# One decoder layer: softplus as four squares, a narrower position bias, and another route from the last batch to its router logits

## The chip, the cores and the metric

The kernel runs on one core of one Trainium2 chip. The metric is the device time of one launch in microseconds (us); lower is better. TensorE (PE in the profile) multiplies matrices, VectorE (DVE) and ScalarE (ACT) do elementwise work, GpSimd (POOL) too, and SyncE (SP) issues most DMAs. Each engine runs its own instructions in order and waits for the others by semaphores.

## The reference, cut to what matters

A post-norm decoder layer over x (4 batches of 256 tokens, width 256) and a context (4 x 256 x 128), in float32.

```
x = layernorm(x + attention(x))          # 32 heads of 8, relative position bias
x = layernorm(x + mamba(context, z=x))   # conv, silu, softplus, scan over 16 states, gate y * silu(x)
# mixture of experts: logits = x @ Wr + br; the best of 4 experts, weighted by its softmax
# expert: (silu(x @ Wg) * (x @ Wu)) @ Wd, 256 -> 1024 -> 256; out = layernorm(x + expert)
```

The position bias of a head is `rel_pos[clip(k - q + 63, 0, 126)].mean()`: it depends on k - q alone and is constant where the distance is 63 or more. The scan's step size is `dt = softplus(v) = relu(v) + log(1 + exp(-|v|))`.

## The kernel before, in words

Every engine has its own program, in an order written out by hand. There are four parts.

The start (0 to 78 us): weights and tokens are turned, queries and keys are projected and written as three bf16 parts each to DRAM (`store_parts`, one call per half of the tokens), from where they come back stacked (`load_stack`, 48 rows a head). Convolution and silu give u, and from that the scan's inputs B, C and dt. VectorE makes the third part of queries and keys (`third_part`, L1351), and then takes the maxima of the first batch's scores (16 units, `maxima`, L1395) with "chores" in between: third parts, `put_u`, and the steps of `softplus(0, step)` (L1374). The logarithm is a polynomial of degree 9 by Horner's rule: one scaling (L1379), eight steps `poly = (poly + c) * e` (L1381) and one addition (L1384), each over 1024 columns, which is half the tokens of both channel blocks. ScalarE's `take_dt` (L1163) makes e = exp(-|v|). After the last chore VectorE clears PSUM (L1564, L1565) and sets `scan_in`, on which ScalarE's first `decay` and GpSimd's first `inject` wait.

The loop (78 to 320 us): 4 batches b of 8 slots qd, each slot for 4 heads and 2 of the batch's 16 scan states m. In a slot TensorE does, four times (i = 0 to 3), the transposed scores of two heads (`scores_b`, L882) and, interleaved, plain scores of two heads of the next half batch, for their maxima (`keys_a` L866, `bias_a` L871). The bias is added by matmuls: `bias_a` multiplies a flip matrix with a Hankel matrix over 512 columns (L872), the bias of `scores_b` is four matmuls of 128 columns, each with its own weights (L901). `weigh` (L907) sums the probabilities times v, `sum_states` (L832) adds a scan state into PSUM by an fp32 identity matmul (L841). ScalarE does the exponentials (L1262) and the scan's decays (L1225). VectorE takes two maxima per state and scans it (L1440); in batch 0, slots 2 to 6, it also does the ten steps of `softplus(1, step)`, for the other half of the tokens. GpSimd multiplies each state's input (`inject`, L608) and output (`weigh_state`, L616), 512 columns each. The eight `tail` steps of a batch (context turned, normalised, projected, added, statistics) run in slots 1 to 4 of the next batch. A unit of TensorE takes the next of two PSUM banks (`turn`) once VectorE has emptied it (`taken`).

The last batch's end (320 to 362 us): `sum_states` ends, then `put_y`, the 8 `tail` steps of batch 3, the scaling (`seed`, `newton`) and `centre` of the first layernorm (L1508), ScalarE's `squash` (L1247), VectorE's `gate` (L1518), `turn_back` (L957), `add_mixed` (L1526), again scaling and `centre`, then the rows are turned (`turn_x2`), copied (`put_x2`) and multiplied with Wr (`route`, `put_logits`). Routing follows on VectorE (L1609 to L1658): one-hot of the best expert, positions by two counting matmuls, a one-hot matrix per token tile (L1647), the row indices. `keep_warm` (L827) issues matmuls without use in between. GpSimd then gathers the rows of 11 tiles (L674) and copies each for TensorE to turn (`hand_row`, `turn_x`).

The experts (362 us to the end): a loop over 11 tiles (L1081 to L1125), which no edit touches.

## Time and profile before

| | us |
|---|---|
| median of 3 runs | 501.59 (497.32 to 502.73) |
| the profiled execution's own time | 503.87 |
| its span, first to last instruction | 501.9 |
| TensorE busy | 448.9 (89%) |
| VectorE busy | 324.1 (65%) |
| GpSimd busy | 222.3 (44%) |
| ScalarE busy | 199.4 (40%) |
| mean granted TensorE clock | 0.954 |

Busy shares are means over parts with different limits, so they have to be read by part. The clock is given as a share of 2.4 GHz: 0.50 is 1.2 GHz. Durations of one instruction include its latency, and neighbours on one engine overlap by some 0.1 us, so the cost of one in a chain is the distance from its start to the next start. The 2 us between span and own time lie outside the instructions.

### The profile page before, as it was taken

What the parts mean: (1) busy time and instruction counts of PE and PEld (TensorE: products, weight loads), DVE (VectorE), ACT (ScalarE), POOL (GpSimd) and SP (SyncE); (2) the same over time, 40 slices, a digit from 0 to 9 for tenths busy, and PEclk for the clock granted to TensorE, in tenths of its full rate; (3) what the DMA queues carried; (4) which work ended last, traced back from release to release, by engine and by line L of the source; (5) the groups of instructions that cost most, each with busy time, mean ns of one, the idle gap of its engine ahead of it and who ended that gap; (6) DMA issues with size and microseconds to landing.
All of it is one profiled execution on the core that took longest, in us unless ns stands there. A gap on an engine that the chain in (4) does not pass through costs nothing.

```text
span 501.9 us, 8238 instructions
## 1 busy us (share of the span) xinstructions
PE 448.9 (89%) x2779; PEld 223.7 (45%) x2780; DVE 324.1 (65%) x621; ACT 199.4 (40%) x392; POOL 222.3 (44%) x239
## 2 busy tenths in 40 slices
PE   5899967977998999999999999878699999999992
PEld 3444222422343444444444443433345665666662
DVE  2696886999987778857888666477302433334344
ACT  1564315645464576635756467211011111121110
POOL 2000109887786789836898579100450111111001
PEclk9999875989899999989999999989989999999997
DMA  8799950243282442914545210394110000000000
GB/s 226 141 233 155 292 178 23 103 90 72 74 143 75 102 99 79 226 52 156 168 166 166 70 44 1 127 368 133 34 51 0 10 10 12 11 10 10 10 2 8
DMA packets 39367, 49.39 MB, mean 98 GB/s; under 512 B 4664, under 2 KB 32673, under 8 KB 39334
## 3 DMA queue, kind: packets, MB, share of 16 engines
q1 hardware_dynamic: 36322, 46.65, 35.0%
q0 software_dynamic: 1056, 2.10, 1.3%
q10 hardware_dynamic: 1956, 0.21, 0.4%
q8 instruction: 20, 0.33, 0.3%
q14 instruction: 13, 0.11, 0.1%
HBM read 40.72 MB, written 8.91 MB: 99 GB/s over the span
## 4 chain that ended last, share of the span: by engine, by line
PE 71%; DVE 17%; issue 5%; POOL 3%; ACT 2%; DMA 1%; POOLq 0%; SPq 0%; DVEq 0%
PE ps L1086 15%; PE ps L841 9%; PE ps L1102 8%; PE ps L872 7%; PE ps L868 7%; PE ps L914 5%; DVE arena L1381 4%; PE ps L901 4%; PE ps L741 3%; DVE arena L1440 3%; DVE arena L1397 3%; PE ps L1094 2%; PE ps L754 1%; PE ps L945 1%; PE ps L953 1%
## 5 line engine op out<-in xcount | busy, mean ns | idle before, releaser
L1262 ACT ACTIVATE arena<-ps 128x512 f32<-128x512 f32 x128 | 76.1, 595 | 101.1 <-PE ps L901 101.0
L1397 DVE TENSOR_REDUCE arena<-ps 128x2 f32<-128x512 f32 x128 | 86.7, 685 | 31.1 <-PE ps L872 28.8
L619 POOL TENSOR_TENSOR arena<-arena 128x512 f32<-128x512 f32 x60 | 76.2, 1270 | 41.5 <-DVE arena L1440 41.5
L613 POOL TENSOR_TENSOR arena<-arena 128x512 f32<-128x512 f32 x64 | 90.5, 1416 | 0.3
L1086 PE MATMUL ps<-arena 128*128 x176 | 79.2, 604 | 0.7 <-ACT arena L1288 0.6
L1440 DVE TENSOR_TENSOR_SCAN arena<-ps,arena 128x512 f32<-128x512 f32 x60 | 72.8, 1213 | 2.3 <-ACT ps L1225 1.2
L841 PE MATMUL ps<-arena,identf 128*128 128x512 f32 x128 | 71.1, 646 | 0.0
L1225 ACT ACTIVATE ps<-arena 128x255 f32<-128x255 f32 x128 | 60.4, 473 | 11.3 <-DVEq L1567 11.3
L868 PE MATMUL ps<-arena 48*128 48x256 bf16 x256 | 51.8, 284 | 14.1 <-ACT arena L1262 7.0
L1665 DVE TENSOR_TENSOR arena<-arena,ps 128x1024 f32<-128x1024 f32 x11 | 13.4, 1221 | 67.9 <-ACT arena L1292 67.9
L872 PE MATMUL ps<-hank_hi,flip 128*128 128x512 f16 x128 | 52.1, 407 | 0.0
L895 PE MATMUL ps<-arena 49*128 49x256 bf16 x256 | 51.2, 281 | 0.1
L901 PE MATMUL ps<-flip,hank 128*128 128x128 f16 x512 | 51.1, 224 | 0.0
L1086 PEld LDWEIGHTS ps<-arena 128*128 128x128 f32 x176 | 33.1, 193 | 39.1 <-issue 39.1
L686 POOL DMA_INDIRECT out<-rows_s,arena x11 | 10.8, 982 | 88.4 <-DVE rows_s L1694 88.4
L868 PEld LDWEIGHTS ps<-arena 48*128 48x128 bf16 x256 | 14.4, 95 | 79.0 <-DVE arena L1397 43.0
L901 PEld LDWEIGHTS ps<-flip,hank 128*128 128x128 f16 x512 | 39.2, 100 | 17.6 <-issue 5.0
L1102 PE MATMUL ps<-arena 128*128 x176 | 39.9, 380 | 1.2 <-ACT arena L1296 1.2
L1292 ACT ACTIVATE arena<-ps 128x1024 f32<-128x1024 f32 x11 | 11.3, 1023 | 67.8 <-PE ps L1086 67.8
L1102 PEld LDWEIGHTS ps<-arena 128*128 128x128 f32 x176 | 32.7, 190 | 5.9 <-issue 1.9
L914 PE MATMUL ps<-arena,vaug 128*9 128x256 f32 x512 | 34.5, 388 | 0.8 <-ACT arena L1262 0.8
L674 POOL DMA_INDIRECT rows_s<-x_d,arena x11 | 11.3, 1031 | 43.4 <-DVEq L1659 40.6
(200 smaller groups left out, 532.9 us busy)
## 6 DMA issues: line engine op xcount, KB each, us to landing
arena<-bc_d SPq DMA_DIRECT2D x32, 512.0 KB, 4.1
arena<-in_L_ffn_Wg SPq DMA_DIRECT2D x8, 512.0 KB, 5.7
arena<-in_L_ffn_Wu SPq DMA_DIRECT2D x8, 512.0 KB, 6.1
arena<-in_L_ffn_Wd SPq DMA_DIRECT2D x4, 1024.0 KB, 11.8
arena<-kp_d SPq DMA_DIRECT2D x8, 384.0 KB, 7.8
arena<-qp_d SPq DMA_DIRECT2D x8, 384.0 KB, 9.7
qp_d<-arena SPq DMA_DIRECT2D x4, 384.0 KB, 10.0
kp_d<-arena SPq DMA_DIRECT2D x4, 384.0 KB, 9.7
```

The lines of the kernel that those rows point to most:

```text
L613: g.tensor_tensor(dBu[m % 3], dtu[:, :, b * SEQ:(b + 1) * SEQ], over_k(bcr[c % BC_RING][:, m % 2, 0, :]), ALU.mult).then_inc(dbu_ready, 1)
L619: g.tensor_tensor(h, h, over_k(bcr[m // 2 % BC_RING][:, m % 2, 1, :]), ALU.mult).then_inc(hc_ready, 1)
L841: mm(ps[:, 7, :], identf[:, :], hst[m % H_RING].rearrange("p k l -> p (k l)"), start=(n == 0), stop=(n == STATES - 1)).then_inc(y_added, 1)
L868: mm(ps[:, bank, i * SEQ:(i + 1) * SEQ], qst[b % 2][lo:lo + ROWS, h, qt * P:(qt + 1) * P], kst[b % 2][lo:lo + ROWS, h, :], start=(i == 0), ...
L872: mm(ps[:, bank, :].rearrange("p (h k) -> p h k", h=2), flip[:, :], hank_hi[:, qt:qt + 1, :].broadcast_to([P, 2, SEQ]), start=False, stop= ...
L901: last = mm(view[:, :, c * QB:(c + 1) * QB], hank2[:, SEQ // QB - 1 - c, kt * P:(kt + 1) * P], flip2[:, :].rearrange("p (o k) -> p o k", o ...
L1086: last = mm(ps[:, b0 + fh, :], xcur[:, k, :], w[:, bass.ds((e * KT + k) * DFF + fh * HALF, HALF)], start=(k == 0), stop=(k == KT - 1))
L1102: last = mm(ps[:, 6, 0:DM], hT[:, f, :], wd_s[:, bass.ds((e * FT + f) * DM, DM)], start=(f == 0), stop=(f == FT - 1))
L1225: A(dA[m % 2][:, k, 1:SEQ], dts[:, k, b * SEQ + 1:(b + 1) * SEQ], ACT.Exp, scale=acol[:, k, n:n + 1]).then_inc(da_ready, 1)
L1262: A(prob[2 * (slot % 2) + kt][:, pr * HALF:(pr + 1) * HALF], ps[:, 2 + n % 2, :], ACT.Exp).then_inc(p_ready, 1)
L1397: v.tensor_reduce(negm[b % 2][:, qt, 2 * pair:2 * pair + 2], ps[:, bank, :].rearrange("p (h k) -> p h k", h=2), axis=AX.X, op=ALU.max).the ...
L1440: v.tensor_tensor_scan(out=h.rearrange(flat), data0=dA[m % 2].rearrange(flat), data1=dBu[m % 3].rearrange(flat), initial=0.0, op0=ALU.mult ...
```

## The change

1. `softplus` works on one batch (512 columns) per step, and log(1 + e) is `e * LEAD * product of four ((e - re)^2 + im^2)`. ScalarE makes the squares (`square`, ACT.Square with a bias), VectorE does four steps `poly = (square + im^2) * poly` and one last step. Batch 0's five steps are chores of the start; those of batches 1 to 3 follow in the loop, one per state for the states 0 to 14. ScalarE's squares of batch 0 stand ahead of `take("low1")`.
2. The far, constant value of the bias is subtracted from the Hankel matrices (softmax takes no notice of it), so that only a band remains: `bias_a` has 384 columns for 512, and L901 becomes three matmuls for four.
3. Start: the third parts of the second half of the tokens are made by GpSimd; the stacks of batch 1 are loaded after the first maxima are sent; part stores have a semaphore each.
4. Steps 0 and 4 of the last batch's tail move into slot 5 of its loop, the other six come ahead of `put_y`.
5. The last batch: the gate multiplies first and takes the tanh, tile by tile, after; the logits are taken from the rows before normalisation (turned right after `add_mixed`, while VectorE computes the scale) and corrected by `rstd * (raw - mean * colsum) + br`; ScalarE copies the turned rows; `centre` follows after the one-hot.
6. Routing: one scan with resets for four, and two PSUM copies gone. TensorE turns the first gathered tile itself, without the copy on GpSimd; six gathers stand ahead of the first copy.

```diff
+LOG1P_LEAD = 0.00523260189
+LOG1P_ROOTS = [(2.321693142115026, 0.6575778587636097), (1.4247407685962707, 1.643811103941353),
...
             def bias_a(bank, b, pair, qt):
-                mm(ps[:, bank, :].rearrange("p (h k) -> p h k", h=2), flip[:, :],
-                   hank_hi[:, qt:qt + 1, :].broadcast_to([P, 2, SEQ]), start=False, stop=True,
+                mm(ps[:, bank, :].rearrange("p (h k) -> p h k", h=2)[:, :, QB * qt:QB * qt + BAND], flip[:, :],
+                   hank_hi[:, qt:qt + 1, :].broadcast_to([P, 2, BAND]), start=False, stop=True,
...
-                for c in range(SEQ // QB):
+                for c in range(kt, kt + BAND // QB):
...
+            for n in range(2):
+                pool.wait_ge(part_ready[n][1], 2)
+                g.tensor_tensor(parts[n][2][:, :, HALF:TOK], rest[n], parts[n][1][:, :, HALF:TOK],
+                                ALU.subtract).then_inc(part_ready[n][2], 1)
...
+                if m % SOFT_STEPS == 2 and 0 < m // SOFT_STEPS < BATCH:
+                    weigh_input(m // SOFT_STEPS)
...
+                        if b == BATCH - 1 and qd == 5 and i % 2 == 1:
+                            tail(b, 4 * (i // 2))
...
-            for step in (0, 1, 4, 5):
+            for step in (1, 5, 2, 6, 3, 7):
                 tail(BATCH - 1, step)
...
+            pe.wait_ge(x2_ready, 2 * (BATCH - 1))
+            turn_late(BATCH - 2)
...
+            route_late(BATCH - 2)
+            keep_warm(12, 5)
             turn_back(BATCH - 1)
+            keep_warm(4, 5)
+            pe.wait_ge(taken, turns.count)
+            turn_late(BATCH - 1)
+            keep_warm(4, 5)
+            route_late(BATCH - 1)
+            keep_warm(14, 7)
...
+            def square(step):
...
+                    act.wait_ge(sp_exp, b // 2 + 1)
+                    if b:
+                        act.wait_ge(sq_used, len(LOG1P_ROOTS) * (b - 1) + i + 1)
+                    A(squares[i], spt[:, :, b * SEQ:(b + 1) * SEQ], ACT.Square, bias=centres[:, i:i + 1]).then_inc(sq_ready, 1)
...
+            for step in range(SOFT_STEPS):
+                square(step)
             take("low1", xdbl[:, half(1)], lambda bank: bank[0:XR, :])
...
+                if step < len(LOG1P_ROOTS):
+                    dve.wait_ge(sq_ready, len(LOG1P_ROOTS) * b + step + 1)
+                    link(v.scalar_tensor_tensor(out=poly, in0=squares[step], scalar=LOG1P_ROOTS[step][1] ** 2,
+                                                in1=poly if step else spt[:, :, cols], op0=ALU.add, op1=ALU.mult))
...
-                        elif b == 0 and 2 <= qd <= 6:
-                            softplus(1, 2 * (qd - 2) + i // 2)
+                        elif m < SOFT_STEPS * (BATCH - 1):
+                            softplus(1 + m // SOFT_STEPS, m % SOFT_STEPS)
...
+                for t in range(2):
+                    link(v.scalar_tensor_tensor(out=lg[:, 2 * b + t, :], in0=colsum, scalar=nwt[:, 2 * b + t:2 * b + t + 1],
+                                                in1=raw[:, t, :], op0=ALU.mult, op1=ALU.add))
...
             dve.sem_inc(oh_ready, 1)
+            dve.wait_ge(late_pe, 4)
+            centre(BATCH - 1, x2_ready)
...
-            turn_x(0)
+            pe.wait_ge(rows_in[0], 16)
+            turn_rows(rows_s[:, 0, :])
```

VectorE at the end of the start, up to the first scan (L1440), before. L1397 is a maximum, L1463 sends maxima, L1381 and L1384 are softplus steps, the MEMSETs clear PSUM:

```order
L1397 TENSOR_REDUCE arena<-ps 128x2 x2
L1381 SCALAR_TENSOR_TENSOR arena<-arena 128x2x512
L1463 TENSOR_SCALAR arena<-ps 8x256
L1381 SCALAR_TENSOR_TENSOR arena<-arena 128x2x512 x5
L1384 TENSOR_TENSOR arena<-arena 128x2x512
L1564 MEMSET ps 128x2 x2
L1565 MEMSET ps 128x512
L1397 TENSOR_REDUCE arena<-ps 128x2
L1440 SCALAR_TENSOR_TENSOR arena<-ps,arena 128x512
```

The same place after the change. L1483 is the maximum, L1555 sends, L1465 and L1469 are softplus steps, L1532 is the scan:

```order
L1465 SCALAR_TENSOR_TENSOR arena<-arena 128x2x256
L1483 TENSOR_REDUCE arena<-ps 128x2 x2
L1469 SCALAR_TENSOR_TENSOR arena<-arena 128x2x256
L1483 TENSOR_REDUCE arena<-ps 128x2 x2
L1555 TENSOR_SCALAR arena<-ps 8x256
L1666 MEMSET ps 128x2 x2
L1667 MEMSET ps 128x512
L1483 TENSOR_REDUCE arena<-ps 128x2
L1532 SCALAR_TENSOR_TENSOR arena<-ps,arena 128x512
```

The six wide steps between the last sending of maxima and the MEMSETs are gone; the steps left are half as wide and all stand between maxima.

ScalarE at the same time, before (L1216 scales u into yT, L1137 takes low1, L1166 and L1167 take dt):

```order
L1137 ACTIVATE vaug<-ps 128x64x8 x2
L1216 ACTIVATE yT<-arena 128x1024 x2
L1137 ACTIVATE arena<-ps 40x512
L1166 ACTIVATE arena<-ps,arena 128x512
L1167 ACTIVATE arena<-ps,arena 128x512
```

And after, the same instructions (L1196, L1284, L1225, L1226) with the squares of batch 0 (L1237):

```order
L1196 ACTIVATE vaug<-ps 128x64x8 x2
L1284 ACTIVATE yT<-arena 128x1024 x2
L1237 ACTIVATE arena<-arena,centres 128x512 x4
L1196 ACTIVATE arena<-ps 40x512
L1225 ACTIVATE arena<-ps,arena 128x512
L1226 ACTIVATE arena<-ps,arena 128x512
```

Four squares now stand ahead of low1 on ScalarE.

VectorE between the last newton step and the first instruction of routing (L1609), before:

```order
L1504 SCALAR_TENSOR_TENSOR rstd<-nwt,rstd 128x2
L1508 TENSOR_SCALAR xres<-xres,mv,rstd 128x256 x2
L1540 COPY arena<-ps 128x512
L1544 TENSOR_TENSOR arena<-ps,br_s 128x8
L1609 TENSOR_REDUCE arena<-arena 128x8
```

And after, where L1712 is the first of routing:

```order
L1593 SCALAR_TENSOR_TENSOR rstd<-nwt,rstd 128x2
L1709 TENSOR_SCALAR nwt<-mv 128x2
L1621 SCALAR_TENSOR_TENSOR arena<-arena,nwt,ps 128x4 x2
L1624 SCALAR_TENSOR_TENSOR arena<-arena,rstd,br_s 128x4 x2
L1712 TENSOR_REDUCE arena<-arena 128x8
```

The two centring steps and the wide copy have left this place; five steps of 2 to 4 columns stand there.

## Rows read from the trace of the kernel before

**Rows 1.** Windows, one per stage: from, to, length, then engines, clock, DMA.

```profile
core 0: us, PE busy (x) PEld busy (x) DVE busy (x) ACT busy (x) POOL busy (x), PEclk, DMA share, GB/s
...
44.00:78.20 34.20, 26.47 (x103) 9.73 (x103) 27.88 (x37) 12.45 (x19) 4.98 (x4) 0.83 0.82 202
78.20:146.00 67.80, 60.93 (x483) 24.61 (x483) 62.68 (x69) 36.40 (x81) 56.72 (x39) 0.89 0.34 82
146.00:208.00 62.00, 59.45 (x527) 26.59 (x527) 50.70 (x79) 36.98 (x81) 50.89 (x54) 1.00 0.49 103
208.00:270.00 62.00, 59.54 (x505) 26.70 (x503) 48.67 (x77) 35.80 (x78) 46.36 (x51) 0.97 0.41 143
270.00:320.70 50.70, 46.68 (x370) 21.34 (x368) 32.46 (x50) 29.47 (x64) 34.24 (x47) 1.00 0.19 62
320.70:362.50 41.80, 30.73 (x225) 16.85 (x223) 26.84 (x103) 3.36 (x6) 4.63 (x5) 0.96 0.58 197
```

**Rows 2.** Timeline of VectorE, end of the start and first scan: start us, us, what.

```profile
67.86 6.26 DVE L1381 SCALAR_TENSOR_TENSOR arena<-arena 128x1024 f32<-128x1024 f32 x5 [0.24 <-DVE arena L1463]
74.15 1.23 DVE L1384 TENSOR_TENSOR arena<-arena 128x1024 f32<-128x1024 f32 x1
...
78.23 1.22 DVE L1440 TENSOR_TENSOR_SCAN arena<-ps,arena 128x512 f32<-128x512 f32 x1 [0.76 <-POOL arena L613]
```

**Rows 3.** Timeline of ScalarE, the same stretch.

```profile
52.72 1.15 ACT L1216 ACTIVATE yT<-arena 128x1024 f32<-128x1024 f32 x1 [2.07 <-DVE arena L1371]
...
56.51 0.59 ACT L1137 ACTIVATE arena<-ps 40x512 f32<-40x512 f32 x1 [0.91 <-PE ps L762]
```

**Rows 4.** Timeline of VectorE, one round of batch 0.

```profile
98.55 0.69 DVE L1397 TENSOR_REDUCE arena<-ps 128x2 f32<-128x512 f32 x1
...
100.87 1.92 DVE L1381 SCALAR_TENSOR_TENSOR arena<-arena 128x1024 f32<-128x1024 f32 x1
102.83 0.69 DVE L1397 TENSOR_REDUCE arena<-ps 128x2 f32<-128x512 f32 x1
```

**Rows 5.** Groups by line and shape, over the whole span.

```profile
L1371 DVE SCALAR_TENSOR_TENSOR arena<-arena 128x512 f32<-128x512 f32 x4 | 2.7, 685 | 0.1
```

**Rows 6.** Chain that ended last, a half slot of batch 1.

```profile
182.96 0.21 PE ps L868
...
183.61 0.22 PE ps L901 x4
183.83 0.91 PE ps L841 x2
184.75 0.21 PE ps L868
```

**Rows 7.** Chain that ended last, from the last batch's scores to the experts.

```profile
328.47 0.17 DVE arena L1544
...
331.12 0.42 DVE xres L1508
...
334.12 0.70 DVE arena L1524
...
340.45 0.42 DVE xres L1508
...
343.96 0.18 DVE arena L1544
...
361.49 0.42 PE ps L1077 x2
```

**Rows 8.** Timeline, the first gather.

```profile
357.08 1.28 POOL L674 DMA_INDIRECT rows_s<-x_d,arena  x1 [40.58 <-DVEq L1659]
```

**Rows 9.** DMA issues by target: engine, count, median us from issue to landing.

```profile
rows_s<-x_d,arena POOLq DMA_INDIRECT x11, 2.7
```

**Rows 10.** Windows of 2 us in batch 0.

```profile
102.00:104.00 2.00, 0.26 (x5) 0.16 (x4) 1.97 (x3) 0.96 (x2) 1.91 (x1) 0.95 0.00 0
104.00:106.00 2.00, 2.00 (x10) 1.00 (x7) 2.00 (x3) 0.61 (x2) 1.28 (x2) 0.50 0.00 0
```

More of the change, by code:

```diff
@@ L184, in decoder_layer @@
         xin = carve(KT * BATCH * PB, KT, BATCH, PB)
+        sq_at = top[0] - KT * BATCH * PB
+        squares = [arena[:, sq_at + HALF * i:sq_at + HALF * (i + 1)].rearrange("p (k l) -> p k l", k=KT)
+              for i in range(len(LOG1P_ROOTS))]
+        assert sq_at + HALF * len(squares) <= top[0]
         u = carve(KT * TOK, KT, TOK)
@@ L508, in _ @@
             store_bc(1)
-            sp.wait_ge(scan_in, 1)
+            set_ones(1)
+            for h in range(2):
+                load_stack(1, h)
             def load_gate_up(dst, src, e):
@@ L1555, in _ @@
                     put_max(0, 0)
[L1556 removed]
+                if n % 2 and chores:
                     chores.pop(0)()
```

254 lines of the change are left out of this document (150 added, 104 removed).

## The prediction

> **What bounds the kernel now.** I read the windows by stage first. Before the first scan, the stretch from 44 us on has TensorE busy 26.5 of 34.2 us at a granted clock of 0.83 [rows 1]. The timeline of VectorE shows what ends it: after the last maxima five softplus steps of 1.25 us (6.26 us) and an addition of 1.23 us run alone, and the first scan comes at 78.23 [rows 2]. In batch 0 (67.8 us) VectorE is busy for 62.7, more than any other stage asks of it [rows 1]. Its timeline shows rounds, one per scan state: two maxima, a scan, a softplus step, with no gap; from 98.55 to 102.83 one takes 4.28 us, of which the step is 1.96 (100.87 to 102.83) [rows 4]. Batches 1 and 2 take 62.0 us each with TensorE busy for 59.5; VectorE has 50.7 and 48.7, GpSimd 50.9 and 46.4 [rows 1]. TensorE bounds them, with GpSimd some 11 us behind. Batch 3 takes 50.7 with TensorE at 46.7. From 320.7 to 362.5 no engine is full: that is a chain of small VectorE steps with trips to TensorE and ScalarE [rows 1, 7]. The experts after 362.5 us are not touched and stay in the sum as they are.
>
> **The start: 78.2 to about 69 us, a gain of 9.0.** Half-wide steps replace wide ones, five for batch 0 instead of ten for half the tokens. All five stand between maxima, where VectorE also loses the two third parts, so that the row of six wide steps behind the last maxima goes: 67.86 to 75.38, 7.5 us [rows 2]. What is late next is the chain on TensorE and ScalarE: low1, dt, the last maxima, the clearing of PSUM, then the first injection. GpSimd's first weighing of the input, which stood behind VectorE's last step, now finds its data ready during the maxima. That is worth about 1.5 more; I take 9.0. Against it: four squares stand ahead of low1 on ScalarE. At 0.59 each (the price of low1's own copy) they are 2.4 us. ScalarE waited 0.91 us for TensorE before low1 and 2.07 before the scaling of u [rows 3], and u comes earlier now, so I cost them at nothing; if the cover is gone the gain is 6.6. The other bound is 12, if the maxima too become faster without third parts. VectorE's first softplus step may wait for a square, about 1.5 us, and hold two maxima behind it; it delays low1 rather than adds to it, and lies within these ends. The third parts on GpSimd: batch 0 prices 512 columns at 56.72/39 = 1.45 us [rows 1], so two of 1024 columns take 5.8 us behind its clearing of rows, and end near 58. SyncE's part stores queue behind them, and behind these the sending of the first maxima, needed near 66. That is covered by 5 us or so; batch 1's stacks, moved behind the maxima, are needed only four slots later.
>
> **Batch 0: 67.8 to 57, a gain of 10.8.** The states 0 to 14 get a step of 512 columns. Alone such a step takes 0.69 [rows 5]; a wide one takes 1.25 alone and 1.96 while GpSimd works beside it [rows 2, 4], so contention adds 0.71 to 1024 columns and, halved, 0.36 to 512: 1.04. A round is then 4.28 - 1.96 + 1.04 = 3.36. Fifteen are 50.4 us; the last state without a step is 2.3, three sendings of maxima with their waits are 2.0: 54.7. I add 2.3 for stretches in which TensorE is at 1.2 GHz. TensorE's own need per state is two quarters of 0.87, one state sum of 0.92 [rows 6] and half a slot's probability sums (about 0.5): 3.15, less 0.22 for the band, 2.93, just under VectorE's. ScalarE gains a square per state, about 0.5 on 2.3 us of work (36.4 us over 16 states [rows 1]). Bounds: 50 us if contention vanished (TensorE then bounds), 67.8 if a half-wide step costs what a wide one did.
>
> The Trainium skill, GPSIMD Engine Reference, "Key points", says that GpSimd shares its SBUF interfaces with VectorE and that they contend where a VectorE instruction has two SBUF inputs. The steps here agree (1.25 alone, 1.96 beside GpSimd). By that rule the third parts moved to GpSimd slow VectorE's steps in the start, which by these rows is at most 5 x 0.36 = 1.8 us and would make the sum 1.8 worse; I leave it out, since most of these steps then stand in gaps.
>
> **Batches 1 to 3: gains of 3.0, 3.0 and 1.5.** A quarter with both kinds of scores takes 182.96 to 183.83, 0.87 us [rows 6], for 4 x 256 + 512 + 4 x 128 = 2048 columns, or 0.425 ns each. The band takes 256 columns away: 0.109. Over 32 quarters that is 3.5 us. Some of it meets waits that stay (2.5 us a batch, GpSimd's gate among them): 3.0. Batch 3 has 16 such quarters and 16 with only the second kind (128 columns, 0.055 each, a quarter of the four matmuls' 0.22 [rows 6]): 2.6, less two tail steps moved in, about 0.55 each on TensorE and VectorE. Bounds for the three together: 0, if GpSimd takes over, and 11, if the dropped weight load of 128 columns costs more than its columns.
>
> **The end: a gain of 7.8.** (a) Ahead of the first scaling VectorE loses two context pairs (0.55 each and a gap), a 512-column copy (0.69 by rows 5) and a small step (0.17 [rows 7]): 2.1. (b) From the first centring to the gate's end was 331.12 to 334.82, with two centrings of 0.42 and 2.8 after them. Now the tanh of the first tile runs beside the second centring and two steps of 0.70 remain: 1.4 saved. (c) From the second centring, 340.45, to the end of the logits, 344.14, it was 3.7 us [rows 7]. In its place stand five small steps at 0.2: 2.7 saved. The turning, copy and products of the raw rows lie beside the scaling (13 steps of 0.2, with the statistics 4 us); they need about 0.7 + 0.7 + 1.1 and eight warming matmuls. If TensorE is at 1.2 GHz there, they end last and cost 0.5 to 1. (d) Routing loses about 0.9 in copies and scans and gains a 0.9 centring: nothing. The last store of x2 is later by that, but needs to land only before the gather, 10 us on. (e) The first gather starts at 357.08 [rows 8] and lands in 2.7 us [rows 9]; TensorE turned the tile at 361.49 [rows 7]. Without the copy it can at 359.8: 1.6 saved. The second copy, now behind six gathers, is needed only after the first tile's 9 us of products. Bounds for the end: 4 and 10.
>
> **The sum**, against the profiled execution's own time (503.87, its span 501.9 and 2 us around it): 503.87 - 9.0 - 10.8 - 3.0 - 3.0 - 1.5 - 7.8 = 468.8. That execution is 2.3 us above the median of the runs shown, 501.59, so the forecast on the median's scale is 466.
>
> **Rivals.**
> *The freed TensorE time in batches 1 to 3 is not paid out.* GpSimd has 50.9 us of work in batch 1, crowded into its second half, and each state's round goes through it. For it: it works with few gaps there. Against: batch 1 loses one input weighing to batch 0, and 11 us are left. Nothing of the 7.5 would come: 474.
> *A half-wide step does not cost half.* If a step's contention is a fixed wait for GpSimd's running instruction (1.45 us), not a share of its own length, a step costs 0.69 + 0.71 = 1.40 and up to 1.96. Batch 0 then gains between 5 and 0: 471 to 477; I price it at 475. Against: nothing direct.
> *Everything pays fully:* bounds near 12, 13, 9 and 9: 459.
> *Slower than before, by the clock.* In batch 0 TensorE stood idle for 1.74 of the 2 us before 104, busy 0.26, and the granted clock fell from 0.95 to 0.50, 1.2 GHz [rows 10]. The new program also makes it wait for VectorE in batch 0, and shorter matmuls make it idle more in batches 1 and 2. At 1.2 GHz each us of TensorE's work costs one more; batches 0 to 2 hold about 47 + 56 + 56 us of it. From 35 + 5 us of such work at the low clock on, beyond before's, the change is slower: all of batch 1, less 3 us of waits, would give 466 + 53 = 519. For it: batch 0 ran at 0.89. Against: batches 1 and 2 ran at 1.00 and 0.97 with the same kind of waits, and batch 0's are to get shorter.
> The Trainium skill, TensorE: Matmul & The Clock Gate, "The HAM clock gate", says that the throttled clock is the default and activity releases it. By that rule this rival needs idle stretches that the new order does not have; the trace agrees, with 1.00 in batch 1 where TensorE is busy 59.5 of 62.
>
> **How the numbers follow.** Chances: the forecast 0.60 (its own range 461 to 471), the loop unpaid 0.17, dear half steps 0.10, everything pays 0.10, slower by the clock 0.03. The range of 456 to 478 reaches over the rivals on both sides but the last. All but the last are faster by far more than 1%, about what a measurement of this kernel can tell from no change: 0.96 faster; I split the rest into 0.02 within 1% and 0.02 slower.
>
> **What would show it.** Right: the first scan at 67 to 71 us; softplus steps of 1.0 to 1.1 us and rounds of about 3.4 in batch 0; batch 0 near 57 us, batches 1 and 2 near 59 with TensorE still the fullest; quarters of 0.76; from the last state sum to the first expert product about 34 us; a first turned tile 2.7 us after the first gather. Wrong: rounds of 4 us in batch 0, GpSimd or ScalarE without gaps there, batches 1 and 2 still at 62, a first scan after 73, a mean clock under 0.9, or VectorE waiting for the raw logits.

## The result, and the profile after

The changed kernel takes 485.33 us (median of 4 runs, 484.25 to 486.2), the kernel before 501.88 beside it: a ratio of 0.969, 95% interval 0.964 to 0.974. It is faster, by 16.6 us. The forecast was 466 with a range of 456 to 478, so the direction was right and the size wrong: half of the gain did not come. The profiled execution took 486.2 us, its span is 484.5.

The windows of the changed kernel, with the borders at the first scans of each batch (the fields are from, to and length, then the engines, the clock and DMA, as in [rows 1]):

```profile
44.00:74.30 30.30, 25.76 (x92) 9.15 (x90) 18.75 (x30) 13.86 (x22) 10.87 (x7) 0.72 0.60 182
74.30:137.50 63.20, 49.32 (x402) 19.51 (x398) 60.07 (x67) 40.07 (x84) 48.84 (x34) 0.93 0.52 97
137.50:195.10 57.60, 53.77 (x457) 23.48 (x456) 47.55 (x75) 34.14 (x75) 45.44 (x44) 0.98 0.51 101
195.10:253.50 58.40, 54.49 (x470) 24.53 (x468) 48.17 (x78) 35.86 (x79) 46.40 (x51) 1.00 0.49 154
253.50:306.10 52.60, 49.42 (x409) 22.34 (x409) 39.47 (x65) 33.25 (x73) 42.31 (x56) 1.00 0.28 87
306.10:346.70 40.60, 31.33 (x240) 19.04 (x238) 26.50 (x99) 6.92 (x14) 5.28 (x11) 0.87 0.60 201
```

These borders differ from those of [rows 1], and that is the first thing to see. Cut by the same rule, at the scans of states 0, 16, 32, 48 and 63, the kernel before reads, behind the first row of [rows 1], which stays:

```profile
78.20:139.40 61.20, 54.33 (x425) 21.90 (x425) 57.16 (x61) 32.23 (x72) 50.97 (x34) 0.87 0.28 74
139.40:198.00 58.60, 56.05 (x489) 25.02 (x488) 48.00 (x75) 34.60 (x77) 47.30 (x45) 1.00 0.44 100
198.00:260.00 62.00, 59.54 (x502) 26.66 (x500) 48.67 (x78) 35.84 (x79) 46.34 (x51) 0.97 0.52 148
260.00:314.00 54.00, 50.76 (x429) 23.08 (x427) 38.77 (x62) 33.15 (x73) 41.67 (x53) 1.00 0.24 82
314.00:362.50 48.50, 36.65 (x261) 19.44 (x259) 28.74 (x105) 6.18 (x12) 6.56 (x13) 0.96 0.50 169
```

By stage, before to after: first scan 78.2 to 74.3 (-3.9); batch 0 61.2 to 63.2 (+2.0); batches 1, 2, 3 by -1.0, -3.6, -1.4; the last batch's end 48.5 to 40.6 (-7.9); the experts 139.4 to 137.8 (-1.6, no edit there). The sum, -17.4, is the difference of the spans, 501.9 to 484.5. Nearly all that was missed lies in the start and in batch 0, the two stages in which the new softplus runs; the 1.6 us missed in batches 1 to 3 are made up by the experts' 1.6, which are no work of the change (clock 0.99 there for 0.97).

VectorE in two states of batch 0. L1483 is a maximum, L1532 the scan, L1465 a softplus step of 512 columns:

```profile
81.42 0.69 DVE L1483 TENSOR_REDUCE arena<-ps 128x2 f32<-128x512 f32 x1
82.03 1.21 DVE L1532 TENSOR_TENSOR_SCAN arena<-ps,arena 128x512 f32<-128x512 f32 x1
83.16 0.67 DVE L1483 TENSOR_REDUCE arena<-ps 128x2 f32<-128x512 f32 x1
83.74 1.39 DVE L1465 SCALAR_TENSOR_TENSOR arena<-arena 128x512 f32<-128x512 f32 x1
85.28 0.69 DVE L1483 TENSOR_REDUCE arena<-ps 128x2 f32<-128x512 f32 x1
```

GpSimd beside it. L647 is `weigh_state`, L641 `inject`, 512 columns each:

```profile
83.32 1.27 POOL L647 TENSOR_TENSOR arena<-arena 128x512 f32<-128x512 f32 x1 [0.92 <-DVE arena L1532]
84.55 1.71 POOL L641 TENSOR_TENSOR arena<-arena 128x512 f32<-128x512 f32 x1
```

A step that takes 0.69 us alone [rows 5] takes 1.39 here, and a state 85.28 - 81.42 = 3.86 us. Read side by side the two engines show more than a price. The scan's end releases GpSimd's L647 at 83.32. VectorE's step starts 0.42 later, and ends at 85.13, which is 0.54 after L647's end at 84.59. And L641, which starts at 84.55, takes 1.71 instead of 1.27. It looks as if each engine stood still until the other's instruction was through. The kernel before has the same pattern: beside the wide step of [rows 4], at 100.87 to 102.79, its GpSimd has

```profile
100.44 1.26 POOL L619 TENSOR_TENSOR arena<-arena 128x512 f32<-128x512 f32 x1 [0.80 <-DVE arena L1440]
101.67 2.25 POOL L613 TENSOR_TENSOR arena<-arena 128x512 f32<-128x512 f32 x1
```

The step ends 1.09 after L619, which is the time of 1024 columns, and L613 takes 2.25 for 1.27. The experiments test this reading.

The start, on VectorE (L1483 maxima, L1555 the sending of maxima):

```profile
49.31 1.29 DVE L1483 TENSOR_REDUCE arena<-ps 128x2 f32<-128x512 f32 x2 [0.88 <-PE ps L901]
52.03 1.93 DVE L1465 SCALAR_TENSOR_TENSOR arena<-arena 128x512 f32<-128x512 f32 x1 [1.43 <-ACT arena L1237]
...
60.98 0.41 DVE L1555 TENSOR_SCALAR arena<-ps 8x256 bf16<-8x256 f32 x1 [3.06 <-PE ps L952]
```

on TensorE:

```profile
54.85 0.60 PE L897 MATMUL ps<-arena 48*128 48x256 bf16 x2 [3.54 <-DVE arena L1483]
...
56.79 3.63 PE L791 MATMUL ps<-arena 128*40 128x512 f32 x4
```

on ScalarE:

```profile
49.21 2.17 ACT L1284 ACTIVATE yT<-arena 128x1024 f32<-128x1024 f32 x2
51.29 2.55 ACT L1237 ACTIVATE arena<-arena,centres 128x512 f32<-128x512 f32 x4
```

and on GpSimd, where L657 makes the third parts:

```profile
51.28 4.66 POOL L657 TENSOR_TENSOR arena<-arena 128x1024 bf16<-128x1024 f32 x2
```

The first square stands behind both copies into yT. VectorE waits 1.43 us for it, with the next maxima behind. So the step comes 0.75 us behind the start of GpSimd's third part and takes 1.93 us for the 0.69 that it takes alone, 1.24 more. TensorE, which needs the maxima's banks, stands for 3.54 us; after that the product for low1 takes 3.63 us, where the same work at the full clock takes 1.91 (a row of it below). The row of six wide steps of [rows 2] is gone as expected, but 3.9 us were gained and not 9.0.

The end, from the chain that ended last, with the lines that answer to [rows 7] and [rows 8]:

```profile
318.12 0.18 DVE veps L1586
...
322.20 0.70 DVE arena L1607
...
328.80 0.23 DVE arena L1621
...
342.49 3.11 DMA rows_s<-x_d,arena
345.74 0.42 PE ps L1131 x2
```

The tanh is off the chain, the logits follow the scale with four small steps (328.80 to 329.82), and the first tile is turned 3.25 us after its gather starts, where it was 361.49 - 357.08 = 4.41.

### The profile page after: what moved, and what is told of

It is laid out like the page before. It is cut to its first block, busy times and chain, and to the rows that moved or that the text cites. A ratio compares the mean times of both kernels' runs of the same rounds, so it can differ in the third digit from the quotient of the medians.

```text
span 484.5 us, 8012 instructions
## 1 busy us (share of the span) xinstructions
PE 427.5 (88%) x2643; PEld 215.6 (45%) x2644; DVE 316.5 (65%) x620; ACT 210.1 (43%) x410; POOL 224.7 (46%) x246
## 4 chain that ended last, share of the span: by engine, by line
PE 61%; DVE 20%; issue 7%; POOL 7%; ACT 2%; DMA 2%; POOLq 0%; SPq 0%; DVEq 0%
PE ps L1144 16%; PE ps L1160 8%; PE ps L870 7%; PE ps L897 5%; DVE arena L1532 5%; PE ps L901 4%; PE ps L943 4%; DVE arena L1465 4%; PE ps L770 3%; DVE arena L1483 3%; POOL arena L641 2%; PE ps L930 2%; PE ps L1152 2%; POOL arena L647 2%; PE ps L783 1%
## 5 line engine op out<-in xcount | busy, mean ns | idle before, releaser
L1336 ACT ACTIVATE arena<-ps 128x512 f32<-128x512 f32 x128 | 76.2, 595 | 90.7 <-PE ps L930 90.5
L1483 DVE TENSOR_REDUCE arena<-ps 128x2 f32<-128x512 f32 x128 | 86.3, 681 | 27.4 <-PE ps L901 23.3
L647 POOL TENSOR_TENSOR arena<-arena 128x512 f32<-128x512 f32 x60 | 76.3, 1272 | 41.6 <-DVE arena L1532 41.5
L641 POOL TENSOR_TENSOR arena<-arena 128x512 f32<-128x512 f32 x64 | 87.1, 1363 | 4.2 <-issue 4.0
L1144 PE MATMUL ps<-arena 128*128 x176 | 77.5, 593 | 0.6 <-ACT arena L1373 0.6
L1532 DVE TENSOR_TENSOR_SCAN arena<-ps,arena 128x512 f32<-128x512 f32 x60 | 72.8, 1214 | 0.5 <-DVE mv L1577 0.2
L870 PE MATMUL ps<-arena,identf 128*128 128x512 f32 x128 | 68.5, 625 | 0.0
L1295 ACT ACTIVATE ps<-arena 128x255 f32<-128x255 f32 x128 | 60.4, 473 | 2.4 <-DVEq L1669 2.4
L717 POOL DMA_INDIRECT out<-rows_s,arena x11 | 10.8, 985 | 88.7 <-DVE rows_s L1798 80.5
L901 PE MATMUL ps<-hank_hi,flip 128*128 128x384 f16 x128 | 44.6, 349 | 0.0
L930 PE MATMUL ps<-flip,hank 128*128 128x128 f16 x384 | 43.6, 224 | 0.0
L1160 PE MATMUL ps<-arena 128*128 x176 | 39.9, 380 | 1.2 <-ACT arena L1381 1.2
L1377 ACT ACTIVATE arena<-ps 128x1024 f32<-128x1024 f32 x11 | 11.3, 1024 | 66.1 <-PE ps L1144 66.1
L930 PEld LDWEIGHTS ps<-flip,hank 128*128 128x128 f16 x384 | 31.6, 100 | 11.3 <-issue 4.2
```

The lines of the kernel that those rows point to most:

```text
L641: g.tensor_tensor(dBu[m % 3], dtu[:, :, b * SEQ:(b + 1) * SEQ], over_k(bcr[c % BC_RING][:, m % 2, 0, :]), ALU.mult).then_inc(dbu_ready, 1)
L647: g.tensor_tensor(h, h, over_k(bcr[m // 2 % BC_RING][:, m % 2, 1, :]), ALU.mult).then_inc(hc_ready, 1)
L870: mm(ps[:, 7, :], identf[:, :], hst[m % H_RING].rearrange("p k l -> p (k l)"), start=(n == 0), stop=(n == STATES - 1)).then_inc(y_added, 1)
L901: mm(ps[:, bank, :].rearrange("p (h k) -> p h k", h=2)[:, :, QB * qt:QB * qt + BAND], flip[:, :], hank_hi[:, qt:qt + 1, :].broadcast_to([P ...
L930: last = mm(view[:, :, c * QB:(c + 1) * QB], hank2[:, SEQ // QB - 1 - c, kt * P:(kt + 1) * P], flip2[:, :].rearrange("p (o k) -> p o k", o ...
L1144: last = mm(ps[:, b0 + fh, :], xcur[:, k, :], w[:, bass.ds((e * KT + k) * DFF + fh * HALF, HALF)], start=(k == 0), stop=(k == KT - 1))
```

## The experiments

Twelve kernels ran, in three groups; each group shares its runs of the kernel before. The medians of the kernel before were 499.84, 501.99 and 499.70 us in the groups and 501.88 beside the changed kernel, so medians of different groups can be set against each other to some 2 us only. e_out and e_one ran twice, the others four times. "Batch 0" is the time from the first scan to the scan of state 16.

| run | median us | ratio to before, 95% | first scan | batch 0 |
|---|---|---|---|---|
| after | 485.33 | 0.969 (0.964 to 0.974) | 74.3 | 63.2 |
| e_out: no loop steps | 469.36 | 0.941 (0.931 to 0.950) | 74.5 | 47.0 |
| e_one: loop steps with one operand | 482.80 | 0.967 (0.959 to 0.976) | 74.8 | 59.2 |
| e_wide: 10 loop steps for 15 | 484.07 | 0.970 (0.963 to 0.977) | 74.6 | 59.2 |
| e_spread: steps at every second state | 483.45 | 0.969 (0.960 to 0.979) | 73.0 | 53.3 |
| e_swap: step right behind the scan | 480.41 | 0.958 (0.954 to 0.963) | 73.7 | 55.6 |
| b_swap: the same in the kernel before | 496.48 | 0.988 (0.983 to 0.994) | 76.3 | 55.1 |
| e_full: the full bias | 493.40 | 0.984 (0.979 to 0.988) | 76.2 | 63.2 |
| e_start: two orders of the start undone | 482.23 | 0.961 (0.956 to 0.966) | 69.4 | 64.7 |
| e_sq: squares first, alone | 480.48 | 0.964 (0.958 to 0.971) | 70.3 | 63.2 |
| a_horner: the softplus undone | 484.61 | 0.972 (0.964 to 0.979) | 78.1 | 60.0 |
| e_best: e_swap and e_start together | 476.40 | 0.956 (0.948 to 0.963) | 71.8 | 56.7 |
| e_bestw: the same with 10 steps for 15 | 474.31 | 0.952 (0.944 to 0.959) | 69.4 | 57.1 |

### What the loop's steps cost: e_out

```diff
-                        elif m < SOFT_STEPS * (BATCH - 1):
-                            softplus(1 + m // SOFT_STEPS, m % SOFT_STEPS)
+                        elif m < SOFT_STEPS * (BATCH - 1) and m % SOFT_STEPS == SOFT_STEPS - 1:
+                            dve.sem_inc(dt_ready, 1)
```

> After the change without the 15 softplus steps of the loop and their squares on ScalarE (batches 1 to 3 keep dt = relu(v) alone, so part of the softplus is left out). After takes 485.3 us, and the states 0 to 14 take 3.9 us each, while batch 1's take 3.60. Theory 1 (VectorE bounds batch 0 with the step, TensorE without): a state falls to about 3.4 to 3.6, batch 0 from 63.2 to 55 to 58 us, and the run takes 477 to 480. Theory 2 (batch 0 is bound by something else, TensorE or GpSimd, and the steps lie beside it): batch 0 stays within 1.5 us of 63.2 and the run at 484 to 486.

Measured: 469.36 us, batch 0 at 47.0. Theory 1 has the direction, but its numbers were too small: 16 us went, not 5 to 8, and the run is 8 us under its window. I had taken TensorE's need in a state of batch 0 from batch 1, which has the tail steps of the batch before in it. The window of this run shows how little batch 0 asks:

```profile
74.50:121.50 47.00, 44.05 (x398) 18.38 (x396) 39.25 (x53) 32.03 (x72) 42.32 (x35) 1.00 0.70 131
```

So 15 steps of 1.54 us from start to next start, 23.1 us, cost 16.2 us of time. VectorE bounds batch 0 with them, TensorE without them, at 2.9 us a state on the mean. The edit takes ScalarE's squares out too; that they are not the cost is shown by e_swap below, which keeps them all.

### Is it the second operand: e_one

```diff
-                    link(v.scalar_tensor_tensor(out=poly, in0=squares[step], scalar=LOG1P_ROOTS[step][1] ** 2,
-                                                in1=poly if step else spt[:, :, cols], op0=ALU.add, op1=ALU.mult))
+                    if b:
+                        link(v.tensor_scalar(poly, squares[step], LOG1P_ROOTS[step][1] ** 2, 0.05, ALU.add, ALU.mult))
```

(and the last step of a batch in the same way; batch 0's own steps stay.)

> After the change, with each of the 15 loop steps as a tensor_scalar of the same 512 columns (the product with the second operand is left out, so the values are not a softplus). Theory 1 (a step waits about 0.7 us because both its operands lie in SBUF beside GpSimd): a step of one SBUF operand takes at most 0.6 us instead of 1.40, and batch 0 falls from 63.2 to 55 to 58 us, run 477 to 480. Theory 2 (any VectorE instruction of this width is slow there, whatever its operands): a step stays at 1.2 to 1.4 us and the run at 484 to 486.

Measured: 482.80 us, batch 0 at 59.2. Theory 1 falls as it was put. VectorE's step and GpSimd beside it:

```profile
83.75 1.13 DVE L1466 TENSOR_SCALAR arena<-arena 128x512 f32<-128x512 f32 x1
```

```profile
83.33 1.27 POOL L647 TENSOR_TENSOR arena<-arena 128x512 f32<-128x512 f32 x1 [0.92 <-DVE arena L1538]
84.55 1.45 POOL L641 TENSOR_TENSOR arena<-arena 128x512 f32<-128x512 f32 x1
```

A tensor_scalar of one SBUF operand takes 1.13 us. It ends at 84.88, 0.28 us after L647's end at 84.60, and the scaling of 1024 columns in the start of the kernel before (L1379) took 0.69 alone, so some 0.35 is its own time at 512, by my estimate. It had waited for GpSimd like the others. Theory 2 falls too, if by less: the step is 0.26 us shorter than with two operands, since its own time is shorter, and the run 1.2 us below its window. What both forms share is the end, a short time behind GpSimd's. That made the lock the theory for the second group.

### Fewer steps, or other states: e_wide and e_spread

```diff
+STEP_AT = [0, 1, 2, 3, 4, 5, 6, 7, 8, 9]
...
-                cols = slice(b * SEQ, (b + 1) * SEQ)
+                cols = slice(b * SEQ, (b + 1 + (b == 2)) * SEQ)
...
-                        elif m < SOFT_STEPS * (BATCH - 1):
-                            softplus(1 + m // SOFT_STEPS, m % SOFT_STEPS)
+                        elif m in STEP_AT:
+                            softplus(1 + STEP_AT.index(m) // SOFT_STEPS, STEP_AT.index(m) % SOFT_STEPS)
```

> After the change with batch 1's steps at states 0 to 4 as they are and those of batches 2 and 3 together, 1024 columns wide, at states 5 to 9: 10 steps for 15. Theory 1 (the wait is a fixed 0.7 us for each instruction): a wide step takes 1.9 to 2.0 us, the steps of batch 0 sum to 17.5 us for 23.1, and the run takes 479 to 483. Theory 2 (the wait grows with the columns, 1.4 us per 512): a wide step takes 2.6 to 2.8 us and the run 484.5 to 487.

Measured: 484.07 us. VectorE:

```profile
96.29 1.94 DVE L1476 SCALAR_TENSOR_TENSOR arena<-arena 128x1024 f32<-128x1024 f32 x1
...
100.69 2.31 DVE L1476 SCALAR_TENSOR_TENSOR arena<-arena 128x1024 f32<-128x1024 f32 x1
```

A wide step costs 1.94 where a half-wide one costs 1.39, so the wait does not grow with the columns; batch 0 fell by 4.0 us to 59.2. The 2.31 is a step that met the whole of a GpSimd instruction, begun 0.03 us ahead of it; the 1.94 met what was left of one begun 0.42 ahead. The run as a whole missed theory 1's window by 1 us. Batch 1 took 59.4 us in this profile at a clock of 0.97, so the profiled run gave 1.7 of the 4.0 back there.

e_spread is the same edit with `STEP_AT = [0, 2, ... 28]` and steps of 512 columns.

> After the change with the 15 steps at every second state (0, 2, ... 28) instead of every state from 0 to 14. Theory 1 (a state with a step is VectorE's at 3.86 us, one without is TensorE's at about 3.4 to 3.6, and two PSUM banks let TensorE run one unit ahead): pairs of states take 7.1 to 7.3 us, batch 0 falls by 2 to 4 us, batch 1 rises by 1 to 2, run 482 to 485. Theory 2 (an exposed step costs the same wherever it stands): batch 0 falls by about 3 us, batch 1 rises by as much, run 485 to 486.5.

Measured: 483.45 us (480.15 to 486.82). Batch 0 fell by 9.9 us to 53.3, and batch 1 rose by 7.5 to 65.1. The run lies in theory 1's window, but both theories missed the sizes: the seven steps that left gave 1.4 us each in batch 0 and cost 1.1 each in batch 1. Why they are so dear there is not shown: VectorE is busy for 54.7 of the 65.1 us, and the clock was 0.92 for 0.98. The sum, -2.4 us in the profile, is no more than the scatter of the runs. Moving steps to other states pays nothing that these runs can tell.

### The lock: e_swap and b_swap

```diff
+                        if i % 2 == 1 and m < SOFT_STEPS * (BATCH - 1):
+                            softplus(1 + m // SOFT_STEPS, m % SOFT_STEPS)
                         for unit in quarter(A_UNITS[b, qd], i):
                             maxima(*unit)
                         if i % 2 == 0:
                             scan(m)
-                        elif m < SOFT_STEPS * (BATCH - 1):
-                            softplus(1 + m // SOFT_STEPS, m % SOFT_STEPS)
```

> After the change with one order changed on VectorE: each of the 15 loop steps stands right behind the scan, ahead of the state's second maximum, instead of behind it. Read so far: the step starts 0.42 us into GpSimd's weigh_state, which the scan's end released, and ends 0.6 to 0.7 us after that instruction does, and a step of one SBUF operand does the same. Theory 1 (the two engines lock each other out of SBUF: a step waits until the running GpSimd instruction ends, and GpSimd's next one waits for the step): the step now starts 0.1 to 0.2 us before GpSimd's instruction and takes 0.65 to 0.8 us, GpSimd's weigh_state takes 1.7 to 2.0, batch 0 falls from 63.2 to 48 to 53 us and the run to 471 to 476. Theory 2 (each step costs 0.7 us more beside GpSimd wherever it stands): step 1.4 us, batch 0 at 62 to 64, run 484 to 487.

Measured: 480.41 us, batch 0 at 55.6. VectorE:

```profile
83.14 1.21 DVE L1532 TENSOR_TENSOR_SCAN arena<-ps,arena 128x512 f32<-128x512 f32 x1
84.27 0.67 DVE L1465 SCALAR_TENSOR_TENSOR arena<-arena 128x512 f32<-128x512 f32 x1
85.08 1.29 DVE L1483 TENSOR_REDUCE arena<-ps 128x2 f32<-128x512 f32 x2
86.29 1.21 DVE L1532 TENSOR_TENSOR_SCAN arena<-ps,arena 128x512 f32<-128x512 f32 x1
...
97.71 1.78 DVE L1465 SCALAR_TENSOR_TENSOR arena<-arena 128x512 f32<-128x512 f32 x1
```

GpSimd:

```profile
84.43 1.63 POOL L647 TENSOR_TENSOR arena<-arena 128x512 f32<-128x512 f32 x1 [0.29 <-DVE arena L1532]
86.02 1.27 POOL L641 TENSOR_TENSOR arena<-arena 128x512 f32<-128x512 f32 x1
...
97.67 1.28 POOL L641 TENSOR_TENSOR arena<-arena 128x512 f32<-128x512 f32 x1
```

The same instruction, with the same operands and GpSimd just as busy, takes 0.67 us where it took 1.39. It now starts 0.16 us ahead of GpSimd's and GpSimd pays (1.63 for 1.27). From scan to scan it is 86.29 - 83.14 = 3.15 us. Theory 2 falls. Theory 1 has the step's time, with 1.63 on GpSimd just under its 1.7 to 2.0, but not what comes of it: batch 0 is 2.6 us over its window and the run 4.4, since five of the sixteen states take 4.0 to 5.1. An exception supports the lock: the step at 97.71 comes 0.04 us behind GpSimd's at 97.67 (a weighing of the input had shifted it), takes 1.78, and ends 0.54 after it, the same distance as in the changed kernel. The gain in the whole run, 4.9 us by the medians, is less than the 7.6 of batch 0: the profiled run took 60.1 us for batch 2 where after's took 58.4, at a clock of 0.97 for 1.00.

> The kernel before the change with the same order changed: its ten steps of 1024 columns right behind the scan. Theory 1 (lock): a step takes 1.05 to 1.2 us instead of 1.93, batch 0 falls from 61.2 by 6 to 9 us, ratio to before 0.981 to 0.989. Theory 2 (fixed price per step): a step stays at 1.9 us, ratio 0.997 to 1.003.

Measured: 496.48 us, ratio 0.988 (0.983 to 0.994). Theory 1 again, at the edge of its window:

```profile
99.80 1.20 DVE L1381 SCALAR_TENSOR_TENSOR arena<-arena 128x1024 f32<-128x1024 f32 x1
```

```profile
99.97 2.16 POOL L619 TENSOR_TENSOR arena<-arena 128x512 f32<-128x512 f32 x1 [0.18 <-DVE arena L1440]
```

All nine loop steps with two operands take 1.20 us, where they took up to 1.93; batch 0 fell by 6.2. The gain of 5.5 us (1.2%) is small, but its interval stays clear of 1. Order alone, without a new formula, took a third of what the whole change took.

The Trainium skill, SBUF — State Buffer, "Who interferes with whom", says just this: the pair of ports that VectorE and GpSimd share is an exclusive lock, which a VectorE instruction with two SBUF inputs takes against a GpSimd one that reads SBUF, and which a tensor_scalar can take in a 2-port mode; reductions never take it, and "Issue order, not op shape, decides who blocks." The runs agree in each point: 0.67 or 1.39 us by order, 1.13 for the tensor_scalar, and maxima at 0.66 to 0.69 wherever they stand.

### The band: e_full

```diff
-                mm(ps[:, bank, :].rearrange("p (h k) -> p h k", h=2)[:, :, QB * qt:QB * qt + BAND], flip[:, :],
-                   hank_hi[:, qt:qt + 1, :].broadcast_to([P, 2, BAND]), start=False, stop=True,
+                mm(ps[:, bank, :].rearrange("p (h k) -> p h k", h=2), flip[:, :],
+                   hank_hi[:, qt:qt + 1, :].broadcast_to([P, 2, SEQ]), start=False, stop=True,
...
-                for c in range(kt, kt + BAND // QB):
+                for c in range(SEQ // QB):
```

> After the change with the full bias again: 512 columns in bias_a and four matmuls of 128 in scores_b, all else as after. Theory 1 (the band gave what batches 1 to 3 gained, 5.9 us in all, and nothing in batch 0, where VectorE is the bound): batches 1 to 3 longer by 5 to 7 us, batch 0 by under 1, run 490 to 493. Theory 2 (batches 1 to 3 gained from elsewhere, or batch 0 gained too): run under 488 or over 495.

Measured: 493.40 us, 8.1 above after. Theory 1 holds by stages, and its run time is missed by 0.4 us. Batch 0 is the same to 0.1 us; batches 1 to 3 are longer by 0.6, 2.0 and 3.5:

```profile
76.20:139.40 63.20, 50.87 (x434) 20.76 (x432) 60.07 (x68) 39.88 (x84) 48.02 (x34) 0.97 0.51 97
139.40:197.60 58.20, 55.64 (x488) 24.88 (x484) 47.98 (x76) 34.23 (x75) 45.76 (x44) 1.00 0.48 101
197.60:257.90 60.30, 57.81 (x502) 26.31 (x500) 48.62 (x77) 35.77 (x79) 46.33 (x50) 1.00 0.52 151
257.90:314.00 56.10, 53.66 (x442) 24.44 (x441) 39.89 (x66) 33.18 (x73) 41.97 (x56) 0.97 0.24 80
```

The other 1.9 us lie ahead of the first scan. The clock blurs the rest: batch 3 ran at 0.97 here and at 1.00 in after, and the kernel before, with the same instructions in that batch, took 54.0 us at 1.00 and 55.6 at 0.97 (in b_swap). So about 1.6 of the 3.5 is the clock, and the band about 1.9. Batch 1 ran at 0.98 in after; in the eight runs with the band and a clock of 1.00 there it took 56.3 to 57.0, for 58.2 here. The band is worth 5 to 6 us in the batches where TensorE is the bound and nothing in the one where VectorE is.

### The start: e_start and e_sq

e_sq moves one piece of ScalarE's program:

```diff
+            for step in range(SOFT_STEPS):
+                square(step)
             act.wait_ge(hank_ready, 1)
             for k in range(KT):
                 act.wait_ge(u_ready, KT + k + 1)
                 A(yT[:, k, :], u[:, k, :], ACT.Copy, scale=dcol[:, k:k + 1]).then_inc(yt_set, 1)
-            for step in range(SOFT_STEPS):
-                square(step)
```

e_start has that edit too, and VectorE makes the third parts of the second half as chores ahead of put_u, instead of GpSimd.

> After the change with two orders of the start undone: ScalarE makes batch 0's squares ahead of its copies into yT, and VectorE makes the third parts of the second half itself, as chores ahead of put_u, as in the kernel before. Theory 1 (the start came out 5 us late because VectorE waited 1.4 us for the first square and 1.2 us for GpSimd's third parts, TensorE stood 3.5 us and then ran at half clock): the stall goes, TensorE keeps its clock, first scan at 69.5 to 72 instead of 74.3, run 481 to 483. Theory 2 (the chores' sum decides, and 2 more of them cost 2.2 us): first scan at 74 to 76, run 485 to 487.

> After the change with ScalarE's squares of batch 0 ahead of its copies into yT, the third parts left on GpSimd. Theory 1 (the late square caused the stall of the start): VectorE's first step no longer waits 1.43 us, first scan at 70 to 72, run 481.5 to 484. Theory 2 (GpSimd's third parts, 4.66 us each, which the chores run against, cause it): first scan at 73.5 to 75, run 484.5 to 486.5.

Measured: e_start 482.23 us with the first scan at 69.4, e_sq 480.48 us with 70.3. Theory 1 of both; e_sq is 1 us under its window, and e_start lost 1.5 us again in batch 0, for a reason that no run tests. In e_sq VectorE waits for no square:

```profile
50.37 1.29 DVE L1483 TENSOR_REDUCE arena<-ps 128x2 f32<-128x512 f32 x2 [0.88 <-PE ps L901]
51.57 0.68 DVE L1465 SCALAR_TENSOR_TENSOR arena<-arena 128x512 f32<-128x512 f32 x1
...
53.61 1.41 DVE L1465 SCALAR_TENSOR_TENSOR arena<-arena 128x512 f32<-128x512 f32 x1
```

and the longest wait of TensorE around there is 0.78 us, with low1 at the full clock:

```profile
53.15 0.39 PE L897 MATMUL ps<-arena 48*128 48x256 bf16 x2 [0.78 <-DVE arena L1483]
...
54.33 1.91 PE L791 MATMUL ps<-arena 128*40 128x512 f32 x4
```

The late square cost 4.0 us at the first scan, and 4.9 by the medians; by the ratios to the runs of the kernel before it is 2.4, so the size is known to some 2 us. In the seven profiles with batch 0's squares late, the first scan comes at 73.0 to 76.2, in the four with the squares first at 69.4 to 71.8. The wait grew on the way: TensorE's stand is 3.54 us with the square late and 0.78 without, where the wait for the square is 1.43 and the longer step behind it 1.24.

That low1 then took 1.72 us longer was in part chance. e_best below has the start of e_start to the letter and no stand over 0.54 us there, and its low1 ran at half the clock:

```profile
54.68 3.63 PE L787 MATMUL ps<-arena 128*40 128x512 f32 x4
```

Its first scan is at 71.8, 2.3 us behind that of e_start. In e_sq the clock fell too, but behind low1, at 59.4, when TensorE had been busy for 5.3 of the last 5.4 us. All seven profiles with the late squares have a slow low1 (2.9 to 3.6 us), so the stand may well bring it on, but it is not the only thing that does.

The third parts matter little once the squares come first: GpSimd's two instructions cost VectorE some 0.7 on one step (1.41 above), doing them on VectorE costs 2.4 us in gaps, and the two runs lie within each other's scatter. In the changed kernel, by its rows, they make 1.24 us of the stand. No run has the squares late and the third parts on VectorE, so how the 4.0 us divide between the two stays open.

### What the new softplus is worth: a_horner

The edit puts the functions `softplus`, `weigh_input` and the two calls of it back as in the kernel before, takes out `square`, and leaves every other edit.

> After the change with only the softplus undone: Horner's ten steps of 1024 columns for each half of the tokens, ten chores at the start and ten steps in slots 2 to 6 of batch 0, no squares on ScalarE. All other edits stay. Theory 1 (the squares gain at the start, where a step costs its own time, and lose in the loop, where each of 15 for 10 steps waits 0.7 us): first scan at 77 to 80 for 74.3, batch 0 at 58.5 to 61.5 for 63.2, run 486 to 490. Theory 2 (the squares are worth nothing or cost time on the whole): run at or under 485.5.

Measured: 484.61 us (483.16 to 486.03), against 485.33 (484.25 to 486.2): the same. By stages theory 1 holds, first scan 78.1 and batch 0 60.0; by the sum theory 2 does. The squares bring the first scan forward by 3.7 us and lengthen batch 0 by 3.2. The forecast had 19.8 of its 35.1 us in these two stages, most of it for the softplus; in the order in which it was made, the new softplus is worth nothing that can be measured. What it would be worth in the order of e_best is open: no run has Horner's steps there.

### The best version: e_best and e_bestw

e_best has the edits of e_swap and e_start, e_bestw those of e_wide in addition.

> After the change with both edits that paid: the loop's steps right behind the scan, and the start with squares ahead of the copies into yT and VectorE making all third parts. Theory (the two lie in different places, 4.9 and 3.1 us by their medians against 485.3, and a state then stands at 3.15 us): first scan at 69 to 70.5, batch 0 at 55 to 57, run 475 to 478.5. Rival (the start's gain is given back in batch 0 by transfers or the clock that set its first states, as 1.5 us of it were in the run with the start alone): run 478.5 to 481.

> The same with 10 steps for 15: batches 2 and 3 together, 1024 columns wide, at states 5 to 9. A step right behind the scan takes 0.67 us at 512 columns and 1.20 at 1024, so the sum is 5 x 0.78 + 5 x 1.3 = 10.4 us for 11.7, and five states fall from 3.15 to 2.3 to 2.6 while five rise to 3.6 to 3.7. Theory (VectorE bounds these states): batch 0 shorter by 1 to 3 us than in the narrow form, run 473 to 477. Rival (TensorE and ScalarE bound the states without a step at about 3, as in the run without steps): batch 0 within 1 us of the narrow form, run equal within 1 us.

Measured: 476.40 and 474.31 us. The first is in the theory's window, though its profiled run had the first scan late, at 71.8, with low1 at half the clock. For e_bestw the rival holds by the stage: batch 0 took 57.1 us against 56.7 (at a clock of 0.88 for 0.94), so ten steps for fifteen brought nothing there. The 2 us between the medians are no more than the runs scatter (474.89 to 478.49, and 472.52 to 475.96). Either is faster than both kernels; e_bestw is at 0.952 of before, where the change alone was at 0.969.

## Why the prediction was wrong, and where it was right

**The start, -9.0 forecast, -3.9 measured.** The row of six wide steps went as reckoned, and the chain that I named as late next (low1, dt, last maxima, clearing) was late next. I also named the wait that broke it: VectorE's first step waits about 1.5 us for a square (1.43 measured). The step that failed is "it delays low1 rather than adds to it, and lies within these ends". It delayed low1 through TensorE, which stood for 3.54 us, and after that low1 ran at half the clock. With the squares first, the scan is at 70.3 (-7.9), with e_start at 69.4 (-8.8). The price of the squares themselves was sized right (2.55 us for 2.4); their place was not: I looked at what they hold up (low1) and not at what they are held up by (2.2 us of copies into yT). The third parts on GpSimd were priced right too, at up to 1.8 us, and left out "since most of these steps then stand in gaps". Two steps paid 1.24 and 0.50 us for them, and the first of these did not stand in a gap but in TensorE's stand.

**Batch 0, -10.8 forecast, +2.0 measured.** Two errors of about the same size make up the 12.8 us.

- The base was wrong. I took 67.8 us for batch 0, from 78.2 to 146.0, and set against it a sum over 16 states. From the first scan to that of state 16 it is 61.2 us; the window held 6.6 us of batch 1, because I had put its border at batch 0's last addition of state sums (put_y), which belongs to the next batch's second slot. Only ten of the sixteen states had a step; the other six took 16.6 us together, four of them 2.3 each. The same kind of sum for the kernel before, ten states of 4.28 and six of 2.3 with the sendings, comes to 59 and not to 67.8; it would have shown the error.
- "Halved, 0.36 to 512: 1.04". The step took 1.39, a state 3.86 instead of 3.36, so 15 states 7.5 us more; the sum came to 63.2 for 57 because some of the allowance for the clock was not used. This is the rival "a half-wide step does not cost half", which had the mechanism (a fixed wait for GpSimd's running instruction) and the price (1.40) to the hundredth, and got a chance of 0.10 with the words "Against: nothing direct". That the wait is the same 0.7 us for both widths follows from the order: either step starts 0.4 us into GpSimd's instruction. The rival's time for the run, 475, was 10 us too low even so, since it was counted from the same wrong base and the same start. The rows for it were in the trace: GpSimd's timeline beside the wide steps, where L613 took 2.25 us for 1.27. I had read VectorE's timeline there and not GpSimd's.

With the measured change of batch 0 in the place of the forecast one the sum is 503.87 - 9.0 + 2.0 (61.2 to 63.2) - 7.5 - 7.8 = 481.6, or 479 on the median's scale. The start's 5 us make up most of the rest.

**Batches 1 to 3, -7.5 forecast, -5.9 measured.** Right in mechanism: e_full shows the band to be worth 5 to 6 us in these batches, and nothing in batch 0. The sizes were too high, and what each batch shows is the clock's doing too. The terms of batches 1 and 2 were 3.0 each; at the full clock the band gives 1.2 to 1.9 and 2.0. Batch 2 gained 3.6 because the kernel before was profiled there at 0.97 (62.0 us; b_swap, with the same instructions at 1.00, took 60.4). Batch 1 gained only 1.0, for after was at 0.98 there. The term for batch 3 was 2.6 for the band less 1.1 for the two tail steps; from 54.0 before at 1.00 and 55.6 (b_swap) and 56.1 (e_full), both at 0.97, and 52.6 after at 1.00, I estimate 1.9 less 0.5. The first rival, GpSimd as the bound, did not come: it has 45.4 of 57.6.

**The end, -7.8 forecast, -7.9 measured.** Right, and the parts with it: the scaling starts 318.12 - 306.13 = 12.0 us after the last scan for 14.6 before (2.6, forecast 2.1); the gate's steps end 4.8 us after that, for 6.3 (1.5, forecast 1.4); from there to the first gather, 22.3 us became 19.6 (2.7, forecast 2.7 for the logits and nothing for the routing); a first tile turned 3.25 us after its gather for 4.41 (1.2, forecast 1.6). TensorE did run at half the clock for the turning, 1.11 us for four transposes, and VectorE still did not wait for the raw logits.

**The rest.** The experts gave 1.6 us that I had put at nothing; their first products took 593 ns each for 604, with the clock at 0.99 for 0.97. No edit touches them, so this is luck. "Slower by the clock" did not come: the mean clock is 0.958 for 0.954. But its premise, that the clock falls where TensorE idles, does not cover all of these traces: e_sq's fell at 59.4 behind 5.4 us of nearly full work.

## What to carry to other kernels

Where VectorE and GpSimd both work out of SBUF, look at both timelines at the same moment and ask who issued first: here, a step put 0.6 us earlier, ahead of a reduction from PSUM that does not mind, took 0.67 us instead of 1.39, and fifteen half-wide steps for ten wide ones meant fifteen such waits for ten. Cut the stages of before and after by the same event, and test the stage's sum on the kernel before first. And where a chain alternates between engines, price a wait of one engine by what it leaves idle on the other: 1.43 us of waiting on VectorE, with a longer step behind it, became 3.54 us on TensorE.
